# A third buffer of softmax weights and a later place for the products with values in a fused attention and experts kernel

## The reference

```
x = x + tanh(g_xattn) * attention(layernorm(x), ctx, ctx)
x = x + tanh(g_ffn) * experts(layernorm(x), router, gate, up, down, shared ...)

attention(q, k, v):            # q, k, v: 16 x 128 x 512, 8 heads of 16 rows
    qk  = einsum('bdm,bdn->bmn', qh, kh) / sqrt(16)
    sm  = softmax(qk)          # 512 x 512 for each of 128 heads
    ret = einsum('bmn,bcn->bcm', sm, vh)
```

## Time and profile before

| | us |
|---|---|
| median of 3 runs | 1143.47 (1143.18 to 1143.86) |
| the profiled execution | 1143.02 |
| its span in the trace | 1141.3 |
| start of O (L869) in step 1 | 55.51 |
| start of O in steps 8 and 26 | 136.50, 347.15 |
| start of O in steps 28, 29, 30, 31 | 370.33, 382.27, 395.82, 413.15 |
| start of the last turn of outputs | 425.49 |

### The profile page before, as it was taken

The page is one execution under the profiler, slowest core; times in us unless marked ns, Lnnn a source line. Parts: engine busy times, 40 slices in busy tenths (PEclk is TensorE's granted clock), DMA queues, the critical chain, the costliest instruction groups (busy, mean ns, idle before and its releaser), DMA issues.

```text
span 1141.3 us, 21457 instructions
## 1 busy us (share of the span) xinstructions
PE 1112.0 (97%) x5718; PEld 745.6 (65%) x5719; DVE 823.6 (72%) x1162; ACT 525.9 (46%) x1055; POOL 607.5 (53%) x597
## 2 busy tenths in 40 slices
PE   3999999999999999999999999999999999999998
PEld 1344444444444446887888878888888888878887
DVE  6799999999999607674535476676766767648787
ACT  1588888888888841111111134444444444421110
POOL 3245655565555324035767447566664756238772
PEclk9999999999999999999999999999999999999999
DMA  9568776777767208956465356757567575433665
GB/s 239 150 173 208 206 223 179 207 202 219 201 187 195 76 19 299 398 172 220 143 216 182 139 158 183 226 178 222 182 197 217 175 236 169 147 101 104 182 195 185
DMA packets 138800, 214.34 MB, mean 188 GB/s; under 512 B 16128, under 2 KB 61696, under 8 KB 138752
## 3 DMA queue, kind: packets, MB, share of 16 engines
q1 hardware_dynamic: 107980, 131.10, 39.9%
q0 software_dynamic: 18016, 61.88, 17.2%
q10 hardware_dynamic: 12756, 20.77, 5.4%
HBM read 117.48 MB, written 91.75 MB: 183 GB/s over the span
## 4 chain that ended last, share of the span: by engine, by line
PE 62%; DVE 0%; ACT 0%; issue 0%
PE score_ps L144 21%; PE score_ps L1721 19%; PE d_ps L1747 9%; PE d_ps L1678 8%; PE o_ps L1678 3%; PE d_ps L1735 1%; PE o_ps L1735 1%; PE o_ps L1630 0%; PE o_ps L1633 0%; DVE y_all L1484 0%; PE score_ps L1642 0%; DVE hid L1581 0%; DVE th L1576 0%; PE o_ps L1650 0%; PE o_ps L1649 0%; ACT th L1337 0%
## 5 line engine op out<-in xcount | busy, mean ns | idle before, releaser
L707 DVE TENSOR_REDUCE maxima<-score_ps 128x2 f32<-128x1024 f32 x256 | 305.5, 1218 | 25.9 <-PE score_ps L815 22.6
L658 ACT ACTIVATE probs<-sb_ps 128x512 f32<-128x512 f32 x512 | 271.5, 604 | 75.5 <-PE sb_ps L842 75.1
L144 PE MATMUL score_ps<-yn_t,w_split 128*128 128x512 f32 x1056 | 254.8, 397 | 0.0
L1721 PE MATMUL score_ps<-w_split,x_split 128*128 x948 | 246.8, 398 | 0.0
L144 PEld LDWEIGHTS score_ps<-yn_t,w_split 128*128 128x128 f32 x1056 | 197.0, 188 | 51.4 <-issue 5.4
L1721 PEld LDWEIGHTS score_ps<-w_split,x_split 128*128 128x128 f32 x948 | 172.1, 188 | 32.5
L842 PE MATMUL sb_ps<-q_stack,places 50*128 50x512 f32 x512 | 173.5, 467 | 2.1 <-ACT probs L658 1.2
L815 PE MATMUL score_ps<-places,q_stack 48*128 48x512 f32 x512 | 149.0, 475 | 21.4 <-DMA q_stack<-q_dram 16.2
L1179 POOL CAST w_split<-w_raw 128x1024 fp32r<-128x1024 f32 x63 | 66.8, 1061 | 176.8 <-POOLq L1279 106.8
L1184 POOL TENSOR_TENSOR w_split<-w_raw,w_split 128x1024 fp32r<-128x1024 f32 x63 | 153.7, 2440 | 4.1
L842 PEld LDWEIGHTS sb_ps<-q_stack,places 50*128 50x128 f32 x512 | 77.8, 188 | 112.7 <-ACT probs L658 96.5
(11 more groups left out here) (155 smaller groups left out, 1224.0 us busy)
## 6 DMA issues: line engine op xcount, KB each, us to landing
xs_dram<-zero SPq DMA_DIRECT2D x1, 20224.0 KB, 58.6
res_dram<-stage ACTq DMA_DIRECT2D x79, 256.0 KB, 2.3
places<-k_dram SPq DMA_DIRECT2D x64, 192.0 KB, 3.6
q_stack<-q_dram SPq DMA_DIRECT2D x64, 192.0 KB, 4.0
stage<-xs_dram SPq DMA_DIRECT2D x160, 64.0 KB, 2.3
h_split<-xs_dram SPq DMA_DIRECT2D x156, 64.0 KB, 2.4
k_dram<-places SPq DMA_DIRECT2D x16, 512.0 KB, 2.9
q_dram<-places SPq DMA_DIRECT2D x16, 512.0 KB, 3.9
```

Source lines behind the costliest of these rows:

```text
L144: mm = pe.matmul(dst[i], w[:, k, f * P:(f + 1) * P], self.yn_t[:, b, k, t * self.SPAN:(t + 1) * self.SPAN], start=(k == 0 and n == 0), sto ...
L658: act.activation(probs[:, c % 2, head(j)[2], :], sb_ps[:, bank_of_score(s, e), :], ACT.Exp, scale=SCALE).then_inc(exp_done, 1)
L707: dve.tensor_reduce(maxima[q % 2][:, :].rearrange("p (h u) -> p u h", u=8)[:, u, :], sa_ps[:, pair_of_unit(q, g, u), :, :], AX_X, ALU.max) ...
L1721: mm = pe.matmul(gu_ps[j], x_split[j][:, b, k, :], w_split[:, bass.ds(at + (a * 3 * ex.PIECE + k * 2 * FE), 2 * FE)], start=(n == 0), stop ...
```

## The change

`probs` gets a third buffer. Chunk 2 of every group goes to buffer 2; chunks 0 and 1 go to buffers (q + c) mod 2 and chunk 3 to buffer q mod 2. The letters of the products move a chunk: **A** is now chunk 2 and **B** chunk 3 of the group before, C and D chunks 0 and 1 of this one, and E is left in the last step only. In `ORDER` a step begins T S A instead of S S T, and the letter of M, with the same eight S and nine T ahead of it, keeps its place; L comes earlier (`TURNED` 15 becomes 13), now ahead of D. ACT's `copy_out` moves behind exponential 3 of a step instead of exponential 2.

In even steps DVE takes the statistics of x ahead of unit 6 and their aggregate ahead of unit 7; in odd steps nothing moves there (statistics of y behind units 6 and 7). In step 0 they come later. SP issues the rows of maxima ahead of the wait for the kept rows and the load of `x_res`. The first expert weights: their loads come behind the rows of maxima in step 28; their upper parts are taken after chunks 2 and 3 of step 29 and chunk 2 of step 30; the lower part of piece 0 is put ahead of the normed rows on POOL in step 29.

```diff
-        probs = sb("probs", [P, 2, HG, D])
+        probs = sb("probs", [P, 3, HG, D])
...
-        OUTPUTS, VALUES, TURNED, LAST = 4, 9, 15, 17
+        OUTPUTS, VALUES, TURNED, LAST = 4, 9, 13, 17
...
+        def probs_of(q, c):
+            return probs[:, 2 if c == 2 else (q + c) % 2 if c < 2 else q % 2, :, :]
...  SP, slot
-                        sp.wait_ge(y_kept[j], 16 * s.r)
-                    sp.dma_start(x_res[j][:, :], x[b]).then_inc(res_loaded[j], 16)
                 if s.before(NG - 1):
                     store_max_rows((s.q + 1) % 4, s.g + 1)
+                if s.known() and s.g == NG - 4:
+                    load_first_chunk()
+                if s.q % 2 == 0:
+                    if s.at_least(4):
+                        sp.wait_ge(y_kept[j], 16 * s.r)
+                    sp.dma_start(x_res[j][:, :], x[b]).then_inc(res_loaded[j], 16)
...  POOL, slot
                     split_maxima((s.q + 1) % 4, s.g + 1)
+                if s.known() and NG - 3 <= s.g < NG - 1:
+                    lower_weights(s.g - NG + 3)
...
                 if has_late(s):
                     reciprocal_deviation(batch_late(s))
                     normed(batch_late(s), 1 if s.q == 1 else 0)
-                if s.known() and s.g == NG - 3:
-                    for i in range(3):
-                        lower_weights(i)
+                if s.known() and s.g == NG - 2:
+                    lower_weights(2)
...  ACT, slot
-                    if j == 0 and (c >= 2 or s.at_least(1)):
-                        act.wait_ge(pv_done, 4 * s.g + c - 1)
+                    if j == 0 and (c == 3 or s.at_least(1)):
+                        act.wait_ge(pv_done, 4 * s.g + (-2, 0, -1, 1)[c])
...
-                    if e == (HG if s.known() and s.g >= NG - 2 else 3) - 1 and s.at_least(1):
+                    if e == HG - 1 and s.at_least(1):
                         copy_out(s.g - 1)
-                    if c >= 1 and j == HG - 1 and s.known() and s.g == NG - 3:
+                    if c >= 2 and j == HG - 1 and s.known() and s.g == NG - 3:
                         act.wait_ge(ex.w_loaded, 48)
-                        upper_weights(c - 1)
+                        upper_weights(c - 2)
+                    if c == 2 and j == HG - 1 and s.known() and s.g == NG - 2:
+                        upper_weights(2)
...  DVE, slot
+                if prepared(s) and not first:
+                    statistics(q // 2, s.r + 1)
                 if s.before(NG - 1):
                     unit(q1, g + 1, 6)
+                if prepared(s) and not first:
+                    dve.wait_ge(bn_done, 2 * s.r + q // 2 + 3)
+                    first_variance(2 * s.r + q // 2 + 2, q // 2)
+                if s.before(NG - 1):
                     unit(q1, g + 1, 7)
...  PE
-            ORDER = "SSTSSTTBTTSSTSSTCTTOMSSTTSTSDTTSSLSTSTE"
+            ORDER = "TSATSSTTSBTSSTTCSSTTOMTSSTTSSLSTTSDSTTS"
...
-            LAST_ORDERS = ("TSTSTSTSBTTTFTFCTOMTTFTFDTTTFTFEL",
-                           "TTTFTFBTTTFTFCOTTTFTFDTTTFTFEL")
+            LAST_ORDERS = ("TSTASTSTSBTTTFTFCTOMTTFTFDTTTFTFL",
+                           "TTAFTTFBTTTFTFCOTTTFTFDTTTFTFEL")
```

More of the change, by code:

```diff
@@ L424, in slot @@
             def slot(s):
-                if s.known() and s.g == NG - 4:
-                    load_first_chunk()
                 if s.before(NG - 2):
@@ L433, in slot @@
                         keep_y(b - 2, j, yn_done, b - 1)
+                if s.before(NG - 1):
+                    store_max_rows((s.q + 1) % 4, s.g + 1)
+                if s.known() and s.g == NG - 4:
+                    load_first_chunk()
+                if s.q % 2 == 0:
+                    if s.at_least(4):
                         sp.wait_ge(y_kept[j], 16 * s.r)
                     sp.dma_start(x_res[j][:, :], x[b]).then_inc(res_loaded[j], 16)
-                if s.before(NG - 1):
-                    store_max_rows((s.q + 1) % 4, s.g + 1)
                 if prepared(s):
@@ L740, in slot @@
                     unit(1, 1, 5)
+                first = s.known() and g == 0
+                if prepared(s) and not first:
+                    statistics(q // 2, s.r + 1)
                 if s.before(NG - 1):
                     unit(q1, g + 1, 6)
+                if prepared(s) and not first:
+                    dve.wait_ge(bn_done, 2 * s.r + q // 2 + 3)
+                    dve.sem_inc(dve_waited, 1)
+                    first_variance(2 * s.r + q // 2 + 2, q // 2)
+                if s.before(NG - 1):
                     unit(q1, g + 1, 7)
-                if prepared(s):
-                    statistics(q // 2, s.r + 1)
                 if has_late(s):
@@ L749, in slot @@
                     unit(q2, g + 2, 0)
-                if prepared(s):
-                    dve.wait_ge(bn_done, 2 * s.r + q // 2 + 3)
-                    dve.sem_inc(dve_waited, 1)
-                    first_variance(2 * s.r + q // 2 + 2, q // 2)
                 if has_late(s):
@@ L757, in slot @@
                     last_variance(batch_late(s))
+                if first:
+                    statistics(0, 1)
+                    dve.wait_ge(bn_done, 3)
+                    first_variance(2, 0)
                 if s.before(NG - 2):
@@ L852, in by_values @@
                 for j in range(HG):
-                    mm = pe.matmul(o_ps[32 * j:32 * j + HD + 1, :], v_t[q % 2][:, c, j, 0:HD + 1], probs[:, c % 2, j, :],
+                    mm = pe.matmul(o_ps[32 * j:32 * j + HD + 1, :], v_t[q % 2][:, c, j, 0:HD + 1], probs_of(q, c)[:, j, :],
                                    start=(c == 0), stop=(c == KC - 1))
@@ L883, in normed_t @@
                 mm.then_inc(ynt_done, 1)
-            ORDER = "SSTSSTTBTTSSTSSTCTTOMSSTTSTSDTTSSLSTSTE"
-            FIRST_ORDER = "SSSSTTSSTSSTSSTSSTTCTTOMSSTTSTSDTTSSLSTSTE"
-            LAST_ORDERS = ("TSTSTSTSBTTTFTFCTOMTTFTFDTTTFTFEL",
-                           "TTTFTFBTTTFTFCOTTTFTFDTTTFTFEL")
+            ORDER = "TSATSSTTSBTSSTTCSSTTOMTSSTTSSLSTTSDSTTS"
+            FIRST_ORDER = "SSSSTTSSTSSTSSTSSTTCTTOMTSSTTSSLSTTSDSTTS"
+            LAST_ORDERS = ("TSTASTSTSBTTTFTFCTOMTTFTFDTTTFTFL",
+                           "TTAFTTFBTTTFTFCOTTTFTFDTTTFTFEL")
             parts = iter(range(16))
@@ L937, in slot @@
                         by_values(q, g, "CDE".index(step))
-                    elif step == "B" and s.at_least(1):
-                        by_values((q - 1) % 4, g - 1, KC - 1)
+                    elif step in "AB" and s.at_least(1):
+                        by_values((q - 1) % 4, g - 1, 2 + "AB".index(step))
                     elif step == "O" and s.at_least(1):
```

2 lines of the change are left out of this document (1 added, 1 removed).

## The result

| | before | changed |
|---|---|---|
| median (lowest to highest), us | 1143.33 (1142.52 to 1143.86), 4 runs | 1164.91 (1160.97 to 1167.01), 4 runs |
| profiled execution, us | 1143.0 | 1167.01, span 1165.3 |
| mean granted clock of PE | 1.00 | 0.975 |

The changed kernel is slower by a ratio of 1.019 [1.0165, 1.0214]. I forecast 1147 with 1152 as the upper end: the direction was right, the size was wrong by 18 us, and the time lies far outside the range.

The account below looks back on a forecast made before the run. PE and DVE were both taken as nearly full, bound by the chain tying them. 1143.0 - 1.2 - 0.3 + 5.2 - 0.7 = 1146.0, with 0.45 for the median and 0.5 for small waits 1147 us; range 1138 to 1152.

Parts of the forecast that it names:

- The walk of a pair of steps: Loop, an odd and an even step timed from unit prices: 23.30 us together, 11.65 a step against 11.70.
- The wait of L: Odd steps of the loop: PE waits 0.8 us ahead of L for the normed rows `yn`.
- The term -1.2 us for the loop: Some 25 steps of 11.65 us against 11.70, PE's gain taken by L's wait and DVE: -1.2 us.
- my list of signs: Expected trace: O starts 11.6 to 11.7 apart, L's odd-step gap 0.8, DVE idle ahead of unit 6, step 29 idle 5 us.
- rival 4: Step 29: half clock behind PE's pause adds at least 1.6 us, up to 3, giving 1149; chance 0.05.
- The term was +5.2: Step 29: `lower_weights(0)` ahead of `yn` on POOL makes L wait until 9.9 instead of 4.7; least +4, most +6 us.
- The maxima's rows: Step 29: SP's new order mends the late rows of maxima, -0.3 us; not late in the loop.
- The end of the phase, steps 30 and 31: A fills waits between T's, and ACT has one piece less before step 30's O: -0.7 us.
- The wait for exponential 3: Loop: PE's 0.4 us wait a step at the T needing exponential 3 goes, with `copy_out` behind it.
- rival 1: Loop faster: L doesn't wait in odd steps, 11.24 us a step, 1136 with step 29; chance 0.15.
- 2: Rival, no change: L's wait is half as long or hidden by DVE, 11.45 us a step, 1142; chance 0.20.
- Rival 3: Slower still: maxima rows late for a step's first T, or unit 6 loses more; 0.2 us a step, 1152; chance 0.12.

Follow-up runs that it names:

- e1: Changed kernel with the statistics of y and their aggregate each taken one unit earlier on DVE in odd steps: 1139.5 us, ratio to before 0.9977.
- e2: Changed kernel with POOL copying the y rows instead of norming them: 1135.14 us.
- e5: Kernel before, in its own order, with three 128x512 copies on POOL holding up the normed rows in odd steps: 1155.51 us.
- e6: Changed kernel with the edits of e1 and e4 together: 1132.1 us, ratio to before 0.9905.
- e12: e6 with the rows of maxima again behind the kept rows and the load of `x_res` on SP's queue: 1132.7 us, ratio 0.9907.
- e13: Kernel before with only ACT's copy of the outputs moved behind exponential 3: 1141.57 us, ratio 0.9984.
- e14: Kernel before with the product of chunk 1 moved behind L and nothing held up on POOL: 1185.47 us.
- e3: Changed kernel with L put back on place 15, behind the product of chunk 1 (D): 1162.58 us.
- e9: Kernel before with the product of chunk 1 moved behind L and two copies on POOL ahead of the normed rows of odd steps: 1208.06 us.
- e15: e6 with one 128x128 copy on POOL ahead of the normed rows in odd steps: 1142.45 us.
- e10: Changed kernel with the order of e3, the edit of e4 and three copies on POOL ahead of the normed rows: 1180.26 us.
- e4: Changed kernel with the lower part of the first expert weights behind the normed rows on POOL in step 29: 1159.83 us, ratio 1.0161.

## Why the prediction was right and wrong

**The walk of a pair of steps** held to some hundredths. It gave 11.79 + 11.51 = 23.30 between the reduces of unit 0, which is 11.97 and 11.33 from O to O; measured without a fall are 11.96 to 12.04 and 11.35 to 11.37. Within the odd step, against the start of unit 0 at 173.38: O at 1.27 (walk 1.27), unit 4 at 6.03 (6.05), unit 5 at 7.67 (7.70), unit 6 at 9.41 (9.43). The wait of L was 0.8 in the walk and is 0.71 to 0.94 in each of the 13 odd steps. The term -1.2 us for the loop measured 20.4 - 20.7 = -0.3. In my list of signs I put DVE's idle time ahead of unit 6 in odd steps; the walk itself had it in even ones, and there it is, 0.48 us at 170.51.

**The step that failed** is the one where the lower clock was counted as a risk of step 29 only (rival 4, 0.05, at most 3 us). I had noted that the trace of before shows a clock of 1.00 throughout, and took that as "no price" for the pauses that my own walk put into every odd step. Those pauses of 0.8 us brought a fall in 10 of 13 odd steps, which cost 2.07 us each, 20.7 us together; without the pauses (e1, e2) the loop has no fall. The price of the pause was right and the state of the engine that it left was not asked for. A price for this was to be had: the earlier trace rows are at full clock, and a stretch of half the speed can be costed from them. As it was, no bound of the loop's term had it in, and the range ended at 1152.

**A rule on pauses.** The traces show falls behind pauses of 0.71 to 0.94 us in a PE that is busy nearly all the rest of the step (11.20 of 11.96 us), and none behind pauses of 1.1 us in e5. The Trainium skill (TensorE: Matmul & The Clock Gate, HAM oscillation) ties falls to pauses between bursts that last too long, and what it calls too long is more than any pause of this loop; and the section behind it (A second HAM failure mode: psum-queue depth-cycling) tells of a kernel that oscillates from frequent short idles between groups of matmuls. For the loop the first rule would allow no fall at all, and it was this one that I weighed, for step 29 alone; the second, told of another kernel and data type, is nearer to what the loop shows, but gives nothing by which e5 and the changed kernel could be told apart. Where the page and these runs differ, the runs decide.

**Step 29.** The queue on POOL was read rightly: `yn` ends 8.25 us behind the aggregate ("some 8"), PE idles 5.74 us ahead of L. The term was +5.2 and the stretch grew by 7.8. The 2.6 between them fit the clock at half behind the pause, which rival 4 had at 1.6 to 3, but no run had this pause without its fall. e6 shows that without either the stretch is 13.65.

**The small terms.** The maxima's rows: -0.3 forecast, nothing measurable in e12. The end of the phase, steps 30 and 31: -0.7 forecast, -1.0 measured. The wait for exponential 3 is gone as told; e13 shows that alone it is worth 1 to 2 us in all, and its waits of DVE suggest that the reduces set the step beside it. The start was wrong in a small way: one product less there, which I put at no net cost, and O of step 1 is 2.6 us earlier. No run took that apart.

**The rivals.** 1 and 2 needed L without its wait, and e1 and e2 show that they priced it fairly: without it the loop's steps are 11.1 to 11.4 (rival 1: 11.24), and with the loss of step 29 in them e1 took 1139.5 and e2 1135.14, where rival 1 said 1136. What decided against them was the wait, as forecast. Rival 3's mechanisms weren't seen.

## What stays open

The chip was not shown to measure any given thing. The runs support that in this loop the clock falls when PE pauses behind a stretch of scores, turns and small transposes without a product, and stays up when a product lies within that stretch or right ahead of the pause. The runs with the copies on POOL, e14 and e3 are one execution each. Two counts are without an explanation: why e9, with the same stretch and pauses as the changed kernel, has falls in 5 of 13 odd steps and not in 10; and why some odd steps of the changed kernel, with pauses of the same length, have none. e9's steps are longer, 13.85 us, and it holds E at the end of a step; neither was varied alone. A stretch made wholly of other matmuls was not tried.

The traces show a regularity in time that bears on both counts. The falls of e9's loop start 81.92 us apart each time, in every third odd step, and those of e15 139.95 us apart, in every sixth, with like pauses between them that have none. So it also seems to matter when a pause comes, and no run moved a pause in time alone.

Outside the loop there are falls that this account doesn't cover: in step 31 of e6 and e13, some 2 us behind a pause of 0.68 us, and in the experts of e9 and e10. Nor is the kernel before free of them in every execution: the mean granted clock of its executions is 0.995 to 1.000.

## What to carry to other kernels

When a change puts a new wait on PE, even one below 1 us in an engine that is 95% busy, price it twice: by its own length, and by a stretch of half clock behind it, and look at what PE ran before the wait. When an order is tightened, find the operand that then comes last and start its chain earlier: here the statistics of y and their aggregate, each moved ahead of one reduce of DVE, turned +1.9% into -0.2%, and with one piece of POOL's queue moved as well, into -0.95%. And an in-order queue that is off the path (POOL's weights ahead of `yn`) becomes the path as soon as its consumer is moved forward.

## What the runs showed of the hardware

- PE's granted clock went from 1.00 to 0.50 for 3.41, 6.83 or 10.24 us at a time, in a kernel whose PE was busy 96% of the span. In an odd step such a fall cost 1.2 to 3 us; in step 29 of e4 some 4.
- At half clock L took 1.06 us instead of 0.66, a product 1.91 instead of 1.05 (e9).
- Pauses of 0.44 us ahead of L were at the start of falls in e15; pauses of 0.95 to 1.11 us in e5's order were not, in 13 odd steps. Three POOL copies of 128x512 took 0.61 us each and, with the waits between them, delayed the normed rows by some 2.3 us.
- A product and L back to back, 1.6 us without new scores, left DVE idle for 0.94 us and cost more (e3, 11.9 to 12.6 us a step) than the wait it was meant to remove.
